# Beginnings of five stages put in another order, and twelve split products for four plain ones in the last stage

## The reference

```python
    x = x + _L0_attn_ref(_layernorm(x, axis=-1), L0_attn_Wq, L0_attn_Wk, L0_attn_Wv, L0_attn_Wo, L0_attn_bq, L0_attn_bk, L0_attn_bv, L0_attn_bo)
    x = x + _L0_xattn_ref(_layernorm(x, axis=-1), ctx_1024, ctx_1024, fside_Bx1xSxS2_0, L0_xattn_Wq, L0_xattn_Wk, L0_xattn_Wv, L0_xattn_Wo, 16)
    x = x + _L0_ffn_ref(_layernorm(x, axis=-1), L0_ffn_norm_weight, L0_ffn_gate_w, L0_ffn_w1, L0_ffn_b1, L0_ffn_w2, L0_ffn_b2)
    x = x + _L1_attn_ref(_layernorm(x, axis=-1), L1_attn_w_qkv, L1_attn_w_out)
    x = x + _L1_xattn_ref(_layernorm(x, axis=-1), ctx_1024, ctx_1024, L1_xattn_Wq, L1_xattn_bq, L1_xattn_Wk, L1_xattn_bk, L1_xattn_Wv, L1_xattn_bv)
    x = x + _L1_ffn_ref(_layernorm(x, axis=-1), L1_ffn_w_q, L1_ffn_w_k, L1_ffn_w_gate, L1_ffn_value_experts, L1_ffn_output_experts)
```

```python
        q = (x @ w_q).reshape(b, n, HEADS, DIM_HEAD).transpose(0, 2, 1, 3)
        k = (x @ w_k).reshape(b, n, HEADS, DIM_HEAD).transpose(0, 2, 1, 3)
        gates = jax.nn.sigmoid((x @ w_gate).reshape(b, n, HEADS, EXPERTS).transpose(0, 2, 1, 3))
        sel = jnp.argmax(gates, axis=-1)
        gm = jax.nn.one_hot(sel, EXPERTS, dtype=x.dtype) * gates
        values = jnp.einsum('bhne,ehdk,bnd->bhnk', gm, value_experts, x)
        ...
        attn = jax.nn.softmax(sim, axis=-1)
        out = jnp.einsum('bhij,bhjk->bhik', attn, values)
        out = jnp.einsum('bhne,ehkd,bhnk->bhnd', gm, output_experts, out)
        return out.sum(axis=1)
```

## Time and profile before

| what | us |
|---|---|
| three timed runs | 3803.07, 3812.09, 3812.07; median 3812.07 |
| the profiled execution, its span | 3811.46, 3809.7 |
| busy in it: PE, DVE, ACT, POOL | 3510.0, 2798.2, 2065.5, 396.6 |
| stages (start to end, about) | a0 22 to 750, c0 750 to 1530, f0 1530 to 1944, l1 1944 to 2263, c1 2263 to 2682, f1 2682 to 3809 |
| clearing transfer of f0, from issue to landing | 34.8 |
| in l1, a batch of POOL's additions, a batch of PE's steps | 11.75, 17.3 |
| first cast of `f_xs` in the batch at 3018, its end | 3016.1 |
| granted clock of PE, 50 to 54 us | 0.57 |

### The profile page before, as it was taken

One profiled execution on the slowest core, in us unless ns is written; L12 is line 12 of the kernel. 1 busy time (PEld: TensorE's weight loads), 2 busy tenths in 40 slices (PEclk: granted clock), 3 DMA queues, 4 the chain that ended last, 5 costly groups with the idle time before them and its releaser, 6 DMA issues. The chain is left out here.

```text
span 3809.7 us, 91322 instructions
## 1 busy us (share of the span) xinstructions
PE 3510.0 (92%) x28322; PEld 2923.4 (77%) x28322; DVE 2798.2 (73%) x8965; ACT 2065.5 (54%) x6485; POOL 396.6 (10%) x582
## 2 busy tenths in 40 slices
PE   6999999899999999339968989999799999999999
PEld 5888888788888888229956666766588888888887
DVE  5666666677777777646659977888788878788786
ACT  5777777677777777325545548888432223222232
POOL 0000000000000000251158302222000000000000
PEclk9999999999999999669989999999899999999999
DMA  3000000010000000442211000000200000000000
...
DMA packets 56108, 109.69 MB, mean 29 GB/s; under 512 B 8368, under 2 KB 27184, under 8 KB 55728
## 3 DMA queue, kind: packets, MB, share of 16 engines
...
## 5 line engine op out<-in xcount | busy, mean ns | idle before, releaser
L2257 DVE TENSOR_TENSOR f_zgT<-f_zT,f_ps_g 128x512 fp32r<-128x512 f32 x512 | 327.1, 680 | 14.0 <-PE f_ps_g L2088 9.9
L639 ACT ACTIVATE c_pr<-c_sm,c_nmx 128x256 f32<-128x256 f32 x512 | 254.5, 499 | 147.3 <-DVE c_nmx L485 147.3
L127 PE MATMUL f_ps_out<-f_out_rounded,f_zgT 128*128 128x256 f32 x1024 | 295.4, 288 | 0.0
L128 PE MATMUL f_ps_out<-f_out_rest,f_zgT 128*128 128x256 f32 x1024 | 289.5, 283 | 0.0
L2210 DVE TENSOR_TENSOR f_gv<-f_ps_v,f_gm 128x512 f32<-128x512 f32 x256 | 175.5, 685 | 154.8 <-PE f_ps_v L129 154.7
L129 PE MATMUL f_ps_out<-f_out_rounded,f_zgT 128*128 128x256 f32 x1024 | 287.9, 281 | 0.0
L639 ACT ACTIVATE a_pr<-a_sm,a_nmx 128x128 f32<-128x128 f32 (+1 forms) x512 | 227.1, 444 | 98.7 <-DVE a_nmx L485 98.7
L485 DVE CUSTOM_DVE_ANT_0 a_sm<-a_ps_s,causal 128x128 f32<-128x128 f32 (+1 forms) x512 | 152.5, 354 | 157.9 <-PE a_ps_s L371 157.8
L485 DVE CUSTOM_DVE_ANT_0 c_sm<-c_ps_s,c_mask 128x256 f32<-128x256 f32 x512 | 186.8, 421 | 87.1 <-PE c_ps_s L371 86.9
L127 PE MATMUL f_ps_v<-f_val_rounded,f_xs 128*128 128x512 f32 x512 | 215.0, 420 | 5.8 <-DVE f_gv L2210 5.8
L2339 ACT ACTIVATE f_pr<-f_sm,f_nmx 128x128 f32<-128x128 f32 (+1 forms) x256 | 114.9, 449 | 185.5 <-DVE f_nmx L2230 185.5
(11 more groups left out here) (384 smaller groups left out, 11240.3 us busy)
## 6 DMA issues: line engine op xcount, KB each, us to landing
f_slot_rows<-f_run POOLq DMA_DIRECT2D x1, 9216.0 KB, 34.8
...
```

What stands on the lines that cost most here:

```text
L127: nc.tensor.matmul(out, sh, mh, start=start, stop=False, **kw)
L128: nc.tensor.matmul(out, sh, ml, start=False, stop=False, **kw)
L639: last = nc.scalar.activation(pr[:, r, i, 0:n], sm[:, j, i, 0:n], ACT.Exp, bias=nmx[:, j, i:i + 1], scale=-1.0, accum_out=sums[:, r, i:i + 1])
L2257: last = nc.vector.tensor_tensor(zgT[:, k % 2, r], zT[:, s % 2, r, :].bitcast(F32).unsqueeze(1).broadcast_to([P, 2, S]), ps_g[:].rearrange ...
```

## The change

It is in six parts. (1) The block ahead of `constants` is gone; ACT requests the pieces in the same block in which SP requests x. DVE measures only the first of the eight parts there, and the other 28 tiles in the slots of a0's first batch (`measure`); their root and reciprocal are taken in slots 6 and 7. ACT loads the table of the root during that block. (2) In a0 and c0 two pieces and not three are split ahead, the first two are rounded ahead of xT, and in the first batch's slots rounding and subtraction stand at the slot's end and not at its front; PE waits for piece s ahead of q and k, and for piece s+1 only ahead of v. (3) In f0 POOL makes its tables first and requests the clearing behind them. (4) In l1 POOL fetches ahead of its mask, DVE adds batch 0's results, and the root's table is loaded early. (5) In f1 DVE and ACT don't wait for POOL's mask at the start, and two pieces are split ahead; DVE's subtraction of the next batch's xT moves up. (6) In f1 the q and k projection is a `product3` from batch 2 on. `qk_rounded` lies where the staging buffers were, `qk_rest` where the plain weights were; ACT and DVE make them in the last two slots of batch 1. The core of the diff:

```diff
+        @block.scalar
+        def _(act):
+            load_first(act)
+            act.wait_ge(c.begun, 1)
+            nc.scalar.activation(spare[:], c.eps[:], ACT.Sqrt)
...
-            for n in range(TILES):
+            for n in range(MEASURED):
...
-    AHEAD = 3
+    AHEAD = 2
+    known = TILES if cross else MEASURED
+    PARTS = {0: (1, 2), 1: (3, 4), 2: (5,), 3: (6,), 4: (7,)}
...
-                    pe.wait_ge(pieces.split, s + 2 - s % 2)
+                    pe.wait_ge(pieces.split, s + 1)
...
+                if not late(b, 1):
+
+                    pe.wait_ge(pieces.split, s + 2 - s % 2)
...
+            def measure(s):
+
+                tiles = lambda at: [n for q in PARTS.get(at, ()) for n in range(MEASURED * q, MEASURED * (q + 1))]
+                for q in PARTS.get(s, ()):
+                    dve.wait_ge(c.x_in[q], 16)
+                for n in tiles(s):
+                    nc.vector.bn_stats(bn_rest[:, n - MEASURED, :], c.x[:, n, :]).then_inc(measured, 1)
+                if tiles(s - 1):
+                    dve.wait_ge(measured, tiles(s - 1)[-1] + 1 - MEASURED)
+                    for n in tiles(s - 1):
+                        last = nc.vector.bn_aggr(c.mv[:, n, :], bn_rest[:, n - MEASURED, :])
+                    if not tiles(s):
+                        last.then_inc(measured, 1)
+
+            def invert_rest():
+                dve.wait_ge(rstd_s, 3)
+                nc.vector.reciprocal(rstd[:, known:], rstd[:, known:]).then_inc(rstd_s, 1)
+
+                dve.wait_ge(rstd_s, 4)
...
-                        pieces.rest(nc, dve, s + AHEAD, s + AHEAD + 1)
...
+                    if not cross:
+                        measure(s)
+                    pieces.rest(nc, dve, s + AHEAD, s + AHEAD + 1)
+                if not cross and not late(b, 1) and s == PAIRS - 1:
+                    invert_rest()
 
             normalise(0)
+            pieces.rest(nc, dve, 0, 1)
             rest_inputs(0)
-            pieces.rest(nc, dve, 0, AHEAD)
...
+            def take_rest():
+                act.wait_ge(measured, TILES - MEASURED + 1)
+                act.wait_ge(rstd_s, 2)
+                nc.scalar.activation(rstd[:, known:], c.mv[:, known:, 1:2].rearrange("p a d -> p (a d)"), ACT.Sqrt,
+                                     bias=c.eps[:]).then_inc(rstd_s, 1)
...
-                        pieces.round(nc, act, s + AHEAD, s + AHEAD + 1)
...
+                    pieces.round(nc, act, s + AHEAD, s + AHEAD + 1)
+                if not cross and not late(b, 1) and s == PAIRS - 2:
+                    take_rest()
+
+            pieces.round(nc, act, 0, AHEAD)
             take_xT(0)
-            pieces.round(nc, act, 0, AHEAD)
...
-            pool.wait_ge(zeroed, 1)
-            pool.dma_start(c.slots.rearrange("n p d -> p n d"),
-                           zeros.unsqueeze(1).broadcast_to([P, NT, D])).then_inc(cleared, 16)
...
+            pool.wait_ge(zeroed, 1)
+            pool.dma_start(c.slots.rearrange("n p d -> p n d"),
+                           zeros.unsqueeze(1).broadcast_to([P, NT, D])).then_inc(cleared, 16)
...
+                fetch(0)
+                make_keep()
+                for b in range(1, B):
...
+            def add_first():
+
+                for i in range(ST):
+                    xt = c.x[:, i, :]
+                    dve.wait_ge(gathered[i], 16 * TOPS)
+                    nc.vector.scalar_tensor_tensor(xt, fetched[:, i, 0, :], c.wt[:, 0, i:i + 1], xt, ALU.mult,
+                                                   ALU.add).then_inc(half_sum, 1)
+                    dve.wait_ge(half_sum, i + 1)
+                    nc.vector.scalar_tensor_tensor(xt, fetched[:, i, 1, :], c.wt[:, 1, i:i + 1], xt, ALU.mult,
+                                                   ALU.add).then_inc(summed, 1)
...
+                nc.scalar.activation(early[:], c.eps[:], ACT.Sqrt)
...
-    AHEAD = 3
+    AHEAD = 2
+    WHOLE = 2
...
+            pool.wait_ge(xn_ready, 1)
...
+                if late(b, WHOLE):
+                    pe.wait_ge(qk_split, s + 1)
+                    if s == 0:
+                        pe.wait_ge(xs_ready, b + 1)
                 for w in range(2):
                     for dc in range(DC):
-                        last = nc.tensor.matmul(ps_qk[:, w * S:(w + 1) * S], w_qk[:, s, w, dc, :], xnT[:, dc, :],
-                                                start=(dc == 0), stop=(dc == DC - 1))
+                        at, first, end = ps_qk[:, w * S:(w + 1) * S], dc == 0, dc == DC - 1
+                        if late(b, WHOLE):
+                            last = product3(nc, at, [t[:, s, w, dc, :] for t in (qk_rounded, qk_rest)],
+                                            [t[:, dc, :] for t in xs], first, end)
+                        else:
+                            last = nc.tensor.matmul(at, w_qk[:, s, w, dc, :], xnT[:, dc, :], start=first, stop=end)
                 last.then_inc(proj, 1)
...
-            dve.wait_ge(made, MADE)
+            dve.wait_ge(root, 1)
+            nc.vector.reciprocal(rstd[:], rstd[:]).then_inc(root, 1)
             dve.wait_ge(root, 2)
-            nc.vector.reciprocal(rstd[:], rstd[:]).then_inc(root, 1)
-            dve.wait_ge(root, 3)
...
+                    if s == STEPS - 1 and k == K - 1 and (not isinstance(b, int) or b + 1 < B):
+                        rest_x(b + 1)
...
+                if not late(b, WHOLE) and b == WHOLE - 1 and s >= 2:
+                    for n in range(2 * s - 4, 2 * s - 2):
+                        dve.wait_ge(qk_round, n + 1)
+                        nc.vector.tensor_tensor(qk_rest[:, n], w_qk[:, n], qk_rounded[:, n].bitcast(F32),
+                                                ALU.subtract).then_inc(qk_split, 1)
...
+                    act.wait_ge(pieces.split, len(pieces.list))
+                    for n in range(2 * s - 4, 2 * s - 2):
+
+                        act.wait_ge(proj, STEPS * b + n + 1)
+                        nc.scalar.copy(qk_rounded[:, n], w_qk[:, n]).then_inc(qk_round, 1)
...
-        small = sb("small", [P, Pieces.STAGES * PIECE])
+        staging = ExitStack()
+        small = staging.enter_context(nc.sbuf_tensor("small", [P, Pieces.STAGES * PIECE], F32))
+        staging.close()
+        qk_rounded = ctx.enter_context(nc.sbuf_tensor("f1_qk_rounded", [P, 4, 2, DC, P], F32R))
```

More of the change, by code:

```diff
@@ L32 @@
 X_PARTS = 8
+MEASURED = TILES // X_PARTS
 LN_EPS = 1e-5
@@ L516, in rest_inputs @@
                 nc.vector.tensor_tensor(flat(xnT[1]), ps_q[:], flat(xnT[0]).bitcast(F32), ALU.subtract).then_inc(xnT_ready, 1)
+                if isinstance(b, int) and b == 0 and not cross:
+                    pieces.rest(nc, dve, 1, AHEAD)
                 if cross:
```

105 lines of the change are left out of this document (62 added, 43 removed).

## The result

The changed kernel took 3788.93 us (median of 6 runs, 3783.43 to 3791.10) where the kernel before took 3807.65 (6 runs in all, 3803.07 to 3812.09): a ratio of 0.9945, 95% interval 0.9935 to 0.9956, some 19 us. It is faster, but by half of the 38.9 us of my sum, and lies 3 us above the top of my range.

A forecast was written before the change was run, and what follows sets the result against it. PE was taken as the bound in f1's steady part, idle PE as the loss at stage starts. 9.5 - 0.5 + 2.9 + 6 + 6 + 15 = 38.9 us off 3811.5 gave 3772.5, range 3758 to 3786.

The forecast's parts named there:

- a0: First stage: an 18.6 us head start from earlier x, partly lost to late work; gain 9.5 us, range 7 to 14.
- the replay: First ten slots of a0 replayed in the new order with old instruction lengths, giving PE's projection starts; also used for c0.
- c0: Stage c0: first projection 3.2 us earlier, but pieces come at slots' ends; a loss of 0.5 us, range -2 to +3.
- the late pieces eat them: Rival on the head starts: a0 gives 1 us and c0 loses 2, total 3782.6 us; chance 0.15.
- f0: Stage f0: POOL's tables, done first, end 3.28 us earlier and free DVE's first `f_t`; gain 2.9 us, 0 to 3.2.
- the clearing transfer's issue holds `f_t`: Rival in f0: POOL's issue of the clearing DMA blocks `f_t`, so f0 gives nothing, total 3775.4 us; chance 0.07.
- the argument for the tables: In f0: `f_t` keeps ordinary length beside indirect DMAs, so the tables, not the clearing DMA's issue, delay it; 2.9 us.
- l1: Stage l1's start: earlier fetches, additions on DVE and a preloaded table; gain 6 us, range 5 to 7.
- f1, start: Start of f1: gates 2.6 us earlier and most of the 4.73 us `f_gv` wait gone; gain 6 us, 3 to 9.
- f1, batches 2 to 15: Twelve split products replace four plain multiplications: 0.30 us less a step, 0.25 at s = 0; gain 15 us, 5.6 to 16.
- PE is the bound and the steps pass the gain on: In f1: with 8 us of PE idle and DVE busy 846.44 of 1049, PE's shorter products shorten every step; 15 us.
- a wait for `f_gv` in every step: Sign in f1 that DVE, not PE, sets the steps once PE's are 0.3 us shorter: `f_ps_v` waits for `f_gv`.

The follow-up runs named there:

- pieces_early: Changed kernel, still two pieces ahead, but rounding and subtraction right behind take_kv and take_q in a0 and c0, not at the slot's end: 0.9894 of the time before.
- best_measure: Changed kernel with pieces behind take_q and take_kv in a0 and c0, three ahead in f1, qk_rest on POOL, a0's 28 tiles measured later: 3764.29 us, 0.9887.
- c0_ahead3: Changed kernel with c0's pieces back at the old places: three split ahead, later ones at the slot's front: 0.9913 of the time before.
- f0_clear_act: Changed kernel with f0's clearing transfer requested from ACT's queue instead of POOL's: 0.9935 of the time before.
- f1_ahead3: Changed kernel with three pieces instead of two split ahead of f1's first slot: 0.9918 of the time before.

## Why the prediction was half right

- **a0** held: the replay's step starts 12.05, 16.2, 21.9, 29.6 and 71.5 (tenth) were 11.6, 16.3, 22.0, 30.6 and 73.7; 8.8 us instead of 9.5. The replay's cause was right too: v waits 7.7 us for pieces, pieces_early wins 5 to 9 us more there, and in best_measure another place for DVE's measuring changes 0.8 us.
- **c0** is the first step that failed. I had the same late pieces in the replay and wrote that v of s = 6 "is no earlier than before". It was later: steps 2, 4 and 6 wait 10.1 us for pieces, where PE in the kernel before waited 5.6 us in all over the same steps, for `c_qT`, and step 7 starts 4.7 us later after the table load than it did. The stage lost 4.7 us and not 0.5. The mechanism was the rival "the late pieces eat them", in the stage for which I had given it 2 us; c0_ahead3 and pieces_early show it: c0 took 778.3 and 775.8 us.
- **f0**: the rival that the clearing transfer's issue holds `f_t` came true for the second batch, while the first batch's two `f_t` got away; 1.5 us (2.5 by the first product on fetched rows), and not 2.9. The step that failed is the argument for the tables, that `f_t` keeps its length beside the indirect transfers: what holds for them doesn't hold for the long direct one. f0_clear_act shows the cause, and that little hangs on it.
- **l1** held: 5.9 us to PE's first instruction, 6.9 in all.
- **f1, start** failed. I counted what DVE and ACT no longer wait for (6.6, measured 9.2 at step 1), and not what AHEAD = 2 with pieces at the slots' ends takes away: 7.2 us of waits. f1_ahead3 gives 7 back, 5.6 of them in batch 0, where the clock was higher too (1.00 in steps 2 and 3 and not 0.88 and 0.89).
- **f1, batches 2 to 15**: the price of a product was right (0.12, 0.30 a step in 41 steps; the term was 0.30). The step "PE is the bound and the steps pass the gain on" failed for 14 of 56: DVE bounds s = 0, where the sum had 14 x 0.25 = 3.5 us and nothing came. I had read DVE's 846 of 1049 us as slack, an average over slots of which one has almost none (busy for 15.71 of 16.77). The sign that I had named for it, a wait for `f_gv` in every step, wasn't the one: PE waits for `f_zgT`, in one step of four. And the copies and subtractions, priced at nothing because "DVE waits for PE" there, cost 2.3 us at batch 2: 0.5 from step 7 to 8, and 1.8 from 8 to 9 by way of ACT. So of the 16 of the sum 12.2 came, and less 2.3 that makes 9.9.
- **The sum**: c1, which had no term, gave 4.2 us by the clock in the profiled pair and hides as much of the miss there. The forecast stood on one execution, which lay 3.8 us above what became the median of six; by luck that made the miss smaller, since 3807.65 - 38.9 is 3768.8 and not 3772.5.
